# Projected heads: copied by ScalarE and added by GpSimd, with the second norm's statistics one step later

## What is computed

```python
h = tokens(x)                                   # patches of three sizes, gathered, embedded, fused
z = layernorm(h)
q, k, v = split(z @ W_attn + b_attn)            # 12 heads of width 16, causal softmax
h = h + softmax(q @ k.T / 4) @ v @ W_proj + b_proj
z = layernorm(h)                                # "second norm"
logits = z @ weights_in.T                       # 21 nodes of a tree, walked 10 deep
h = h + coefficients(gelu(logits), signs) @ weights_out
```

## Time and profile before

| | |
|---|---|
| time, median of 3 runs | 324.56 us (324.44 to 325.06) |
| the profiled execution's own time | 324.9 us |
| its span | 323.2 us |
| PE busy | 268.2 us (83%) |
| DVE busy | 240.4 us (74%) |
| ACT busy | 202.4 us (63%) |
| POOL busy | 196.5 us (61%) |
| row maxima on VectorE, line 933, 384 | 111.8 us |
| exponentials, line 616, 144 | 81.8 us |
| causal cuts, line 400, 144 | 66.4 us |
| DMA engines, hardware queue q1 | 33.7% |

### The profile page before, as it was taken

One profiled execution on the slowest core, in us unless ns is written; L12 is line 12 of the kernel. 1 busy time (PEld: TensorE's weight loads), 2 busy tenths in 40 slices (PEclk: granted clock), 3 DMA queues, 4 the chain that ended last, 5 costly groups with the idle time before them and its releaser, 6 DMA issues.

```text
span 323.2 us, 7904 instructions
## 1 busy us (share of the span) xinstructions
PE 268.2 (83%) x2506; PEld 196.8 (61%) x2506; DVE 240.4 (74%) x1156; ACT 202.4 (63%) x429; POOL 196.5 (61%) x419
## 2 busy tenths in 40 slices
PE   0499887188787789999999999999989989999872
PEld 0465655077765466666666666667657578777662
DVE  2053887147496839999999999999989988876872
ACT  2653293047346918868778877876865854868770
POOL 3737777500204827778687778688668666556561
PEclk9999999679999959999999999999999999999997
DMA  5822332003970942444434534524432333000039
GB/s 126 235 54 39 85 69 44 16 2 77 130 89 31 125 119 30 114 84 102 125 85 101 129 87 99 127 90 100 110 102 88 110 103 52 2 4 3 0 107 285
DMA packets 27456, 28.13 MB, mean 87 GB/s; under 512 B 7186, under 2 KB 26704, under 8 KB 27416
## 3 DMA queue, kind: packets, MB, share of 16 engines
q1 hardware_dynamic: 23912, 24.56, 33.7%
q0 software_dynamic: 1568, 2.36, 3.2%
q10 hardware_dynamic: 1936, 0.72, 0.9%
HBM read 4.62 MB, written 3.15 MB: 24 GB/s over the span
## 4 chain that ended last, share of the span: by engine, by line
PE 41%; DVE 20%; POOL 14%; issue 9%; DMA 6%; SPq 5%; ACT 4%; POOLq 0%; ACTq 0%; DVEq 0%
POOL G L373 9%; DVE C L933 9%; PE bank L1497 6%; PE bank L1441 5%; SPq L320 4%; PE bank L1475 4%; PE bank L1412 3%; PE bank L1437 2%; PE bank L1500 2%; DMA G<-x,I 2%; POOL PT L400 2%; PE bank L1382 2%; PE bank L1530 2%; ACT PT L616 2%; PE bank L1479 2%
## 5 line engine op out<-in xcount | busy, mean ns | idle before, releaser
L933 DVE CUSTOM_DVE_ANT_0 C<-bank,MASKV 128x256 bf16<-128x256 f32 (+1 forms) x384 | 111.8, 352 | 18.8 <-PE bank L1441 11.2
L616 ACT ACTIVATE PT<-bank 128x512 f32<-128x512 f32 x144 | 81.8, 602 | 40.2 <-PE bank L1475 32.1
L400 POOL TENSOR_SCALAR_AFFINE_SELECT PT<-PT 128x256 f32<-128x256 f32 x144 | 66.4, 473 | 0.0
L396 POOL TENSOR_TENSOR CARRY<-CARRY 1x1 f32<-1x1 f32 x96 | 17.6, 183 | 46.7 <-ACT PT L616 46.7
L378 POOL TENSOR_TENSOR PART<-RES,PART 128x256 bf16<-128x256 f32 (+1 forms) x31 | 28.0, 904 | 21.1 <-ACT PART L610 21.1
L373 POOL DMA_INDIRECT G<-x,I x32 | 30.3, 947 | 14.2 <-issue 9.4
L1497 PE MATMUL bank<-PT,VA 128*32 128x256 f32 x384 | 30.7, 390 | 4.6 <-POOL PT L400 4.6
L933 DVE DVE_READ_ACCUMULATOR2_ANT MX<- 128x1 f32 x384 | 32.2, 84 | 0.0
L946 DVE SCALAR_TENSOR_TENSOR RES<-bank,BQK,PART 128x256 f32<-128x256 f32 x48 | 21.5, 478 | 1.1 <-ACT PART L604 1.1
L604 ACT ACTIVATE PART<-bank,BQK 128x256 bf16<-128x256 f32 x48 | 21.0, 481 | 1.8 <-PE bank L1397 1.8
L1441 PE MATMUL bank<-KS,QS 96*128 96x256 bf16 x96 | 18.6, 275 | 2.0 <-DVE MX L933 1.8
(11 more groups left out here) (181 smaller groups left out, 625.1 us busy)
## 6 DMA issues: line engine op xcount, KB each, us to landing
QS<-PART SPq DMA_DIRECT2D x48, 96.0 KB, 3.6
KS<-PART SPq DMA_DIRECT2D x48, 96.0 KB, 3.6
KSL<-PART SPq DMA_DIRECT2D x48, 96.0 KB, 3.4
QSL<-PART SPq DMA_DIRECT2D x48, 96.0 KB, 3.7
out<-HT SPq DMA_DIRECT2D x7, 384.0 KB, 3.6
G<-x,I POOLq DMA_INDIRECT x42, 4.7
RW<-ZW SPq DMA_DIRECT2D x16, 36.0 KB
WA<-wa SPq DMA_DIRECT2D x1, 432.0 KB, 4.0
```

Of the source, the lines that this page charges most:

```text
L400: pool.affine_select(out=e, in_=e, compare_op=ALU.is_ge, fill=0.0, base=0, pattern=[[0, n], [1, P]], channel_multiplier=-1).then_inc(cut_o ...
L616: nc.scalar.activation(PT[:, v, :], BANK[T_BANK[(SU * par + v) % 2]][:, :], ACT.Exp, scale=SCALE).then_inc(exp_ok, 1)
L933: ins = nc.vector.tensor_tensor_reduce(JUNK[:, n:n + keys], bank[:, j * keys:(j + 1) * keys], MASKV[:, S - keys:S], 1.0, LOWEST, ALU.add, ...
```

## The change

Images 0 to 11, whose residual sum falls into steps 2 to 13, get it in another way. ScalarE copies the projection out of bank MA into a new SBUF tile PJ (`projected`), between its last exponential and `middle` (0). GpSimd adds PJ to the tokens (a new `residual` of its own), last in its step. VectorE's `residual` in `step` is gone; the last four images keep it. The statistics of image b - 3 are taken in step b, between row maximum 4 and the first `rest`; the first closing step takes those of image 11, after row maximum 3. TensorE's third `weighted` group waits for ScalarE's copy (`pv_ok`) where it waited for the sum, except in the last images. The copy waits until GpSimd has added the one before.

```diff
--- before.py
+++ after.py
@@ -126,6 +126,7 @@
         ON = sb("ON", [P, (S + P) // SQ, SQ])
         ONT = sb("ONT", [P, S + P])
         H2 = sb("H2", [P, TT, D])
+        PJ = sb("PJ", [P, TT, D])
         ST2 = sb("ST2", [P, TT, 6])
 
 
@@ -221,7 +222,7 @@
             sem(n) for n in ("sum_ps", "wic_ok", "tree_init", "lga_ok", "lgd_ok", "sl_ok", "slc_ok", "x2d_ok")]
         gn_ok, pw_ok = sem("gn_ok"), sem("pw_ok")
         oc_ok, op_ok, od_ok = sem("oc_ok"), sem("op_ok"), sem("od_ok")
-        st2_ok, mv2_ok = sem("st2_ok"), sem("mv2_ok")
+        st2_ok, mv2_ok, pv_ok = sem("st2_ok"), sem("mv2_ok"), sem("pv_ok")
         ld_ones = sem("ld_ones")
         bpv_ps, bpv_ok, hb_ok = sem("bpv_ps"), sem("bpv_ok"), sem("hb_ok")
         x2t_ps, x2t_ok, lg_ps, ge_ok, tree = [
@@ -421,6 +422,13 @@
                 pool.tensor_tensor(rest, OB[:, 2, :, 0:HS].rearrange("p (t b) d -> p t b d", t=TT),
                                    RC[:, 2, :].rearrange("p (t b a) -> p t b a", t=TT, a=1).broadcast_to([P, TT, P // SQ, HS]), ALU.mult).then_inc(on_ok, 1)
 
+            def residual(b):
+
+                pool.wait_ge(pv_ok, b.off + 1)
+                pool.wait_ge(hb_ok, b.off + 1)
+                hv = HT[:, TT * b.off:TT * (b.off + 1), :]
+                pool.tensor_tensor(hv, PJ[:, :, :], hv, ALU.add).then_inc(h2_ok, 1)
+
             def step(b):
                 f = b + 2
                 if not b.first:
@@ -439,6 +447,8 @@
                     normalise(b - 1)
                 if f.off < B:
                     low(f, 1)
+                if 2 <= b.off < B - 2:
+                    residual(b - 2)
 
             low(Image(0, 0), 0)
             low(Image(0, 1), 0)
@@ -614,6 +624,12 @@
                 if not b.first and v % 3 == 0:
                     act.wait_ge(av_ps, (b - 1).count(3, v // 3 + 1))
                 nc.scalar.activation(PT[:, v, :], BANK[T_BANK[(SU * par + v) % 2]][:, :], ACT.Exp, scale=SCALE).then_inc(exp_ok, 1)
+
+            def projected(b):
+
+                act.wait_ge(pj_ps, b.off + 1)
+                after(act, h2_ok, b.off)
+                nc.scalar.copy(PJ[:, :, :], BANK[MA][:, 0:2 * D].rearrange("p (t d) -> p t d", t=2)).then_inc(pv_ok, 1)
 
             def maxima(b):
 
@@ -656,6 +672,8 @@
                     first_part(f, 1)
                 exp(d, 1 - par, 7)
                 exp(d, 1 - par, 8)
+                if b.off >= 2:
+                    projected(b - 2)
                 if has_front:
                     middle(f, 0)
                 if has_ahead:
@@ -1004,21 +1022,19 @@
                 row_max(b, par, 2)
                 row_max(b, par, 3)
                 row_max(b, par, 4)
+                if b.off >= 3:
+                    residual_statistics(b - 3)
                 if has_front:
                     rest(f, 0)
                 row_max(b, par, 5)
                 row_max(b, par, 6)
                 row_max(b, par, 7)
                 row_max(b, par, 8)
-                if has_old:
-                    residual(b - 2)
                 if has_front:
                     rest(f, 1)
                 heads_by_token(d, False)
                 heads_by_token(d, True)
                 over_sums(d)
-                if has_old:
-                    residual_statistics(b - 2)
 
             def closing_step(b, par):
                 d = b - 1
@@ -1487,6 +1504,8 @@
                 if g == 2:
                     if b.first:
                         pe.wait_ge(r_ok, 7)
+                    elif b.off <= B - 4:
+                        pe.wait_ge(pv_ok, b.off)
                     else:
                         pe.wait_ge(h2_ok, b.off)
                 if g == 0:
```

## The result

The changed kernel takes 330.2 us (median of 4 runs, 329.93 to 331.26), the one before 324.74 us beside it (324.44 to 325.06): 1.0174 times as long, with 1.0148 to 1.02 as the 95% interval. It is slower, as forecast, but by 5.5 us instead of 2.8, and outside the range, which ended at 329.4. The profiled execution took 329.93 us. In the later experiments the executions of every kernel, the one before included, fall in two groups some 5 us apart; both kernels are compared here within the faster one.

The account below looks back on a forecast made before the run. A chain of waits through GpSimd, TensorE and VectorE bounds the step at 11.73 us. Adding 0.24 and 0.07 a step over 11 steps, with stalls and closing step adjusted, gave +2.8 on 324.56: 327.3 us, range 324.2 to 329.4.

Parts of the forecast that it names:

- Removing `residual` from VectorE: In each middle step: gains 0, since the reciprocals wait for the third `weighted`; the freed 0.7 us become idle time.
- the 0.75 us taken from the step's start: Statistics leaving VectorE's step start: row maximum 2 comes only 0.25 us earlier, held by scores 2; the rest turns idle.
- the new place: Between row maximum 4 and the first `rest`: row maximum 5 ends 0.50 us later, against 0.26 of cover ahead of scores 7.
- ScalarE's copy: Ahead of `middle` and `front`: delays `front`, `max_t` and the third `weighted`, +0.07 us a step, bounds 0 and 0.2.
- The add: Last in GpSimd's step: 0, taken from idle time ahead of the first cut, 0.75 us of cover left.
- Rivals 1 and 2: First, freed VectorE time counts, 322.4 to 324 us; second, everything is hidden, 324.5 to 325.1 us; chance 0.12 each.
- rival 3: Heavy case: GpSimd's shared port, or a slower copy making the maxima transfer late; 330 to 336 us, chance 0.05.
- The step that failed: Stalls over the 11 middle steps: longer steps swallow part of the 1.16 us, some 0.8 stay.
- Statistics: Moving them within VectorE's step: 0.50 us of delay less 0.26 of cover ahead of scores 7, +0.24 us a step.
- The row sum in the prediction: Copy's delay through `front` and `max_t` to the third `weighted`: +0.09 us, or +0.05 with the quickest semaphores.
- The first closing step: After the 11 steps: its opening stall of 0.95 us shrinks by 0.3, statistics moved there cost about 0.1.
- what lies around it, unchanged: Outside the span of the profiled execution: 1.7 us, taken as unchanged.

Follow-up runs that it names:

- e1: Against the kernel before, only the statistics move (image b - 3, after row maximum 4), VectorE keeping its residual sum; clean step 12.01 us, ratio 1.0108.
- e3: The changed kernel with ScalarE's copy placed behind `front` instead of ahead of `middle` and `front`; clean step 12.01 us, ratio to the kernel before 1.0146.
- e9: e3 with GpSimd's add done twice, the first into a spare tile; clean step 12.01 us, ratio to the kernel before 1.0101.
- e4: e3 with the statistics moved into VectorE's idle time after the second `rest`; clean step 11.53 us, ratio to the kernel before 1.0013.
- e7: e4 with SyncE stacking part 2 of queries and keys last; 326.37 us, clean step 11.53 us, ratio to the kernel before 0.9928.
- e2: The changed kernel with the statistics (still of image b - 3) at their old place behind `over_sums`; clean step 11.83 us, ratio to the kernel before 1.0025.
- e8: The changed kernel with the statistics in VectorE's idle time after the second `rest`, copy still early; clean step 11.65 us, ratio to the kernel before 1.0027.
- e6: The changed kernel with SyncE stacking part 2 of queries and keys last; clean step 12.12 us, ratio to the kernel before 1.0037.
- e5: The kernel before with only SyncE's stacking order changed, part 2 of queries and keys last; 322.1 us, ratio 0.9853.

## Why the prediction was right in kind and short in size

**Right.** The clean step, link by link, in us after W (predicted from rows 3 to 7, measured in the step of W = 202.13):

| link | predicted | measured |
|---|---|---|
| reciprocals | 1.41 | 1.40 |
| row maximum 2 | 4.11 | 4.11 |
| scores 7 | 8.30 | 8.34 |
| scores 8 | 9.40 | 9.45 |
| `middle` (0) | 11.14 | 11.17 |
| `front` | 11.43 | 11.48 |
| `max_t` | 11.95 | 12.00 |
| next W | 12.04 to 12.06 | 12.12 |

Removing `residual` from VectorE was worth nothing; of the 0.75 us taken from the step's start only 0.25 arrived; and the new place met a cover of about 0.25 for 0.5 of delay. ScalarE's copy delayed `front` and through it `max_t` and the third `weighted`. The add was free. e1, e3 and e9 single these out. Rivals 1 and 2 are out for the place chosen: scores 7 did not have 0.5 us of cover. Rival 1's gain of 0.20 a step exists, and e4 and e7 show it, but only with the statistics elsewhere. The 330.2 us lie in the 330 to 336 of rival 3, and yet its mechanism isn't what happened: no VectorE operation is longer beside an add, and the late transfer of the maxima makes nobody wait for it, but for the one wait of 0.6 us that the kernel before has too; it delays what is queued behind it (point 3 below).

**The step that failed** is "Of the 1.16 us of stalls, a step that is 0.31 longer swallows the small ones and 0.31 of each big one, since the stacks start at a fixed distance from W; some 0.8 stay". 1.60 us are there, twice that. Two premises of it were wrong, points 3 and 4 below. Beside it two terms of the clean step were too small by 0.04 us each.

**The terms that were mis-sized.**

1. *Statistics, 0.24 predicted, 0.28 measured.* I moved them with the 0.75 us that they take at the old place. At the new one `rest` follows 209.28 - 208.47 = 0.81 us behind their start. With that the sum gives 8.36 for scores 7 (measured 8.34). 11 x 0.04 = 0.4 us.
2. *Copy, 0.07 predicted, 0.11 measured (12.12 against e3's 12.01).* The row sum in the prediction said 0.09; I took the mean of it and a variant with the quickest semaphores, on no row's evidence. 11 x 0.04 = 0.4 us.
3. *The stacks don't keep their distance from W.* Here the mechanism is at fault, not a size. I wrote that ScalarE's `maxima` and SyncE's transfer of them come some 0.35 later, and counted 0, looking only at who reads the transfer. I did not ask what stands behind it in SyncE's queue: the first stacking transfers of the next step. In the timeline of SyncE after, with W = 202.13, the transfer is issued at W + 0.58 instead of W + 0.10 (210.75 above):

```profile
202.71 0.65 SPq L327 DMA_DIRECT2D QS<-MT  x1
203.47 1.83 SPq L321 DMA_DIRECT2D KSL<-PART  x3
206.03 2.28 SPq L321 DMA_DIRECT2D QSL<-PART  x3
```

   The second group of stacking issues starts at W + 3.90 in both kernels, since it waits for `low`; so the hole in the queue takes up the delay of 0.48 itself. But three issues that took 1.82 us take 2.28 here, and the last one starts at W + 9.46 instead of 8.96; why they take longer, no run here tells. It comes with the late transfer: the last of the twelve transfers lands at W + 12.98, 13.14 and 13.04 (medians of 11 steps) in the three kernels that have it and the old order (after, e2, e8), and at 12.64 to 12.85 in the five that don't (before, e1, e3, e4, e9). Measured from the next W the last landing comes 0.84 behind it in the kernel before and 0.81 in the kernel after, so that nearly nothing is swallowed; in e1, e3 and e9 it is 0.62 to 0.68, so there the longer step does swallow. e1 has 3 steps in 11 over its clean duration, e3 has 2, e9 4, the kernel after has 7 (before: 4).

4. *A cover that went unnoticed.* In the kernel before, a step whose scores 0 start late is longer by that lateness less 0.21 (0.28 late costs 0.07, 0.44 costs 0.23, 1.03 costs 0.82), since row maximum 2 waited for VectorE at W + 4.36 anyway. With row maximum 2 at 4.11 that cover is gone: steps whose scores 0 start 0.11 and 0.12 late (W = 140.49 and 226.41, scores 0 at 0.90 and 0.91) are 0.17 and 0.11 longer, one of 0.83 is 0.82 longer. (One of 0.20, at W = 251.09, is only 0.08 longer.) Over the 11 steps scores 0 are late by 2.4 us in sum before and by 1.7 after. Had each late step of the kernel after still had 0.21 of cover, its lateness would have cost 0.75 us, which is the forecast's 0.8. So by this sum the lost cover makes up the miss, and point 3 shows in the number of late steps and in where the stacks land; it is an argument from one profile of each kernel, and no run separates the two. Points 3 and 4 together turn the forecast's -0.35 into +0.44: 0.8 us. Single stalls of 0.6 to 1.4 us come in every kernel with the old order, and e1, e3 and e9, which transfer the maxima as early as the kernel before, have sums of 1.55, 0.73 and 1.42. So the +0.44 alone is within what kernels alike in this vary by, while the 7 disturbed steps lie outside their 2 to 4. One in the kernel after:

```profile
177.93 0.76 issue
```

5. *Around the 11 steps.* The step from W of step 1 to that of step 2 grew by 0.28 us (16.64 to 16.92). I had not costed it, having begun to count at step 2. e1 has 16.63 and e3 16.66 there, e2 17.02, which speaks for the early copy; but e4 and e9 have 16.76 and 16.77 with the late one and e6 16.75 with the early one, so the cause is open. The W of step 1 itself is 0.10 earlier, which leaves +0.18. The first closing step gave back 0.43 where I counted 0.2. And "what lies around it, unchanged" missed the +0.4 at the last output transfer.

Sum of the misses: 0.4 + 0.4 + 0.8 + 0.2 - 0.2 + 0.4 = 2.0 of the 2.1 us between a predicted +2.8 and the +4.9 of the spans. The rest up to 5.5 is mostly that the profiled execution after (329.93) is the fastest of its 4 runs and the one before (324.9) is not.

**The range** ended at 329.4 and was made from bounds of ScalarE's share, with no bound for a delayed queue of SyncE outside rival 3, where it had 0.05.

## What to carry to other kernels

Price a moved instruction by the slack of its new place, and recompute every cover behind it: on an engine of 94% busy time, removing one operation gained nothing, and moving another cost 0.28 in one place and, with the first removed, gained 0.20 in another. When an edit delays a transfer, look at what is queued behind it on its issuing engine and not only at who reads it. And look for stalls in that queue's order first: here the order of six calls was worth more (11 steps 1.2 us shorter, the closing step 0.9) than any placing of VectorE's work found here short of combining both.

## What the runs showed of the hardware

**TensorE's clock in the first full step.** From W of step 1 to that of step 2 takes 16.5 to 17.0 us in nine kernels, but 14.95 in e5 and 15.17 in e8. The stretch from 117 to 121 us in the kernel before and in e5 (columns as in rows 1):

```profile
117.00:121.00 4.00, 4.00 (x22) 3.14 (x21) 0.97 (x5) 1.09 (x2) 0.00 (x0) 0.56 0.67 144
```

```profile
117.00:121.00 4.00, 3.97 (x31) 2.75 (x30) 2.66 (x17) 2.70 (x6) 1.36 (x5) 0.96 0.86 138
```

The granted clock is 0.56 in the one, near the lower level of 1.2 GHz, and 0.96 in the other, nearly all at 2.4 GHz; a pair of line 1475 takes 0.63 us against 0.38. TensorE is busy all along in both. Why the clock rises earlier in e5 is open: e8 has the old stacking order and shows it, e6 and e7 have the new one and don't. So some 1.7 us of e5's gain in its span can't be credited to the order; the 1.2 and 0.9 can.

**A DMA issue has no fixed price.** The same stacking issue takes 0.55 to 0.65 us in most places and in others 1.0 to 2.3 (W = 226.41: one issue at W + 7.05, the next at 8.89). Where they come isn't all chance: behind the W of step 10, of step 11 and of step 12 there is such an issue in all eleven kernels. In the eight with the old order the last stack behind these then lands at W + 12.8 to 14.0, in most cases at 13.3 or later, and the stretch from W of step 11 to that of step 12 is over the clean duration in all eight, by 0.3 to 1.4 us. What causes it, no run here tells.

**The 5 us between the places of W of step 1 are TensorE's speed early on.** In every profile TensorE starts its first 16 matmuls at 11.0 to 11.9 us and needs 3.4 to 3.6 us for them. The next 16, in the kernel before and in e9, from TensorE's timeline:

```profile
15.63 1.95 PE L1319 MATMUL bank<-G2T,W2S 96*64 96x256 f32 x16 [0.67 <-ACT G2T L525]
...
19.97 1.99 PE L1242 MATMUL bank<-ID,G 128*96 128x128 f32 x16
```

```profile
15.32 3.68 PE L1338 MATMUL bank<-G2T,W2S 96*64 96x256 f32 x16 [0.67 <-ACT G2T L537]
...
22.89 3.65 PE L1261 MATMUL bank<-ID,G 128*96 128x128 f32 x16
```

The same instructions with the same wait ahead take 1.95 us or 3.68, and the transposes behind them 1.99 or 3.65, so GpSimd's next gathers, which wait for these, begin at 22 or at 27 us. The granted clock of the windows is 1.00 in both, so here that column doesn't tell them apart; the durations do. The five profiles with the early W of step 1 have 1.95 and the other six 3.68. What decides it, no run here tells.
